# The threshold search of an expert-choice router, moved from a phase of its own into the batches of a linear attention

## What is computed

```python
# branch 1, linear attention (per sequence; then two layer norms and an MLP)
Q = elu(xn @ Wq + bq) + 1;  K = elu(xn @ Wk + bk) + 1;  V = xn @ Wv + bv
KV = einsum('bshd,bshm->bhdm', K, V)
Z  = 1 / (einsum('bshd,bhd->bsh', Q, K.sum(axis=1)) + 1e-6)
attn_out = einsum('bshd,bhdm,bsh->bshm', Q, KV, Z).reshape(b, s, 1024) @ Wo + bo
# branch 2, expert choice
scores = softmax(xn @ router_w + router_b)      # 4096 tokens x 8 experts
G, idx = top_k(scores.T, 256)                   # each expert takes its 256 best tokens
# gather, two matmuls with relu, weigh by G, add back to the tokens
x = x + s * silu(g)
```

## Time and profile before

| | us |
|---|---|
| median of 3 runs | 3729.77 (3727.99 to 3736.72) |
| the profiled execution | 3725.95 |
| its span, first to last instruction | 3724.1 |
| granted TensorE clock, mean over the span | 0.805 |
| PE busy over the span | 2474.6 (66%) |
| DVE busy over the span | 2064.1 (55%) |
| ACT busy over the span | 1371.2 (37%) |

### The profile page before, as it was taken

The page is one execution under the profiler, slowest core; times in us unless marked ns, Lnnn a source line. Parts: engine busy times, 40 slices in busy tenths (PEclk is TensorE's granted clock), DMA queues, the critical chain, the costliest instruction groups (busy, mean ns, idle before and its releaser), DMA issues. The chain is left out here.

```text
span 3724.1 us, 58202 instructions
## 1 busy us (share of the span) xinstructions
PE 2474.6 (66%) x19990; PEld 1767.7 (47%) x19990; DVE 2064.1 (55%) x4703; ACT 1371.2 (37%) x2383; POOL 825.8 (22%) x793
## 2 busy tenths in 40 slices
PE   5989941634250489804169999998615296968994
PEld 3655631522050488702145555557513275956773
DVE  4555566354919234264778888883345695442115
ACT  3444410322300023012148888883214332423432
POOL 0000001210057121073042000001344871113200
PEclk9999975775655699557579999998857697977997
DMA  5000000210021236310000000004410003731100
GB/s 170 1 1 0 0 2 14 65 28 3 0 54 37 46 122 206 89 41 4 19 28 20 1 1 1 1 1 146 146 35 25 20 0 114 221 95 36 32 0 28
DMA packets 156415, 172.87 MB, mean 46 GB/s; under 512 B 55333, under 2 KB 125738, under 8 KB 155594
## 3 DMA queue, kind: packets, MB, share of 16 engines
q1 hardware_dynamic: 135322, 127.39, 12.0%
q0 software_dynamic: 20912, 43.22, 3.9%
HBM read 124.61 MB, written 45.94 MB: 46 GB/s over the span
## 5 line engine op out<-in xcount | busy, mean ns | idle before, releaser
L2451 DVE CUSTOM_DVE_ANT_0 decayed_sd<-decayed_sc,decayed_decay 128x512 f32<-128x512 f32 x512 | 331.7, 686 | 86.0 <-PE decayed_sc L2328 85.8
L2406 ACT ACTIVATE decayed_pr<-decayed_sd,decayed_shift 128x512 f32<-128x512 f32 x512 | 339.0, 713 | 49.2 <-DVE decayed_shift L2458 49.0
L2340 PEld LDWEIGHTS decayed_tr<-all_ident,decayed_pr 128*128 128x128 f32 x2048 | 223.6, 140 | 175.1 <-ACT decayed_pr L2406 101.0
L2340 PE MATMUL decayed_tr<-all_ident,decayed_pr 128*128 128x128 f32 x2048 | 276.8, 278 | 11.0 <-ACT decayed_pt L2413 10.8
L450 PE MATMUL experts_up<-experts_xt,experts_w 128*128 128x256 f32 x1140 | 272.8, 386 | 0.0
L450 PEld LDWEIGHTS experts_up<-experts_xt,experts_w 128*128 128x128 f32 x1140 | 212.2, 195 | 24.7
L207 PE MATMUL norm_turned<-all_ident,norm_xn 128*128 128x128 f32 x128 | 35.7, 435 | 266.9 <-DVE norm_xn L143 266.9
L2465 DVE COPY decayed_pt<-decayed_tr 128x512 f32<-128x512 f32 x256 | 173.2, 685 | 2.6 <-PE decayed_tr L2340 2.6
L427 POOL DMA_DIRECT2D rows_out<-experts_y x121 | 87.4, 723 | 364.8 <-DVE experts_y L512 199.8
L376 POOL DMA_INDIRECT rows_in<-L_T,all_slot x128 | 149.5, 1168 | 83.0 <-issue 38.4
L684 PEld LDWEIGHTS moe_down<-moe_w,moe_h 128*128 128x128 f32 x1024 | 131.8, 192 | 56.3 <-issue 55.3
(11 more groups left out here) (508 smaller groups left out, 5578.5 us busy)
## 6 DMA issues: line engine op xcount, KB each, us to landing
experts_w<-in_L_experts SPq DMA_DIRECT2D x78, 384.0 KB, 3.3
experts_w<-in_L_experts SPq DMA_DIRECT2D x43, 579.0 KB, 4.0
experts_tok<-rows_in SPq DMA_DIRECT2D x121, 128.0 KB, 3.4
rows_out<-experts_y POOLq DMA_DIRECT2D x121, 128.0 KB, 3.4
fir_band<-bands SPq DMA_DIRECT2D x16, 768.0 KB, 7.4
rows_in<-linear_zero SPq DMA_DIRECT2D x43, 128.0 KB, 1.8
experts_w<-in_L_experts SPq DMA_DIRECT2D x8, 514.0 KB, 3.5
experts_b<-in_L_experts_b SPq DMA_DIRECT2D x43, 64.0 KB, 4.2
```

Source lines behind the costliest of these rows:

```text
L2340: last = pe.transpose(tr[u % TURNED][:, t * P:(t + 1) * P], pr[:, u % RING, t * P:(t + 1) * P], m.ident[:, :])
L2406: act.activation(pr[:, u % RING, :], sd[:, u % RING, :], ACT.Exp, bias=shift[:, u % RING:u % RING + 1]).then_inc(exp_ready, 1)
L2451: dve.tensor_tensor_reduce(out=sd[:, u % RING, :], in0=sc[h][:, :], in1=decay[:, qt, :], scale=1.0, scalar=-3.0e38, op0=ALU.mult, op1=ALU. ...
```

## The change

The search moves out of the choice phase. A class `Search` holds its buffers over both phases. The softmax and the first `propose` (L941 to L945 of the changed kernel) run on DVE before the first `join_q`, with the softmax's Exp first on ACT. The 15 counts and 15 decisions are spread over the 8 batches: one decision after V, one after the joins of the next Q; batch 0 has only the second. A decision of rounds 1 to 14 ends with the next round's `propose`; the last one does not. The counts are matmuls into the bank `y`, which is free until the output projection of the batch. All 8 batches are now written out, there is no loop and no register offset in the attention; `xb` and POOL's copies go, and PE takes the weights of K and V from `m.XNT`. SP stores `score` behind the zeroing. The choice phase starts at what was L1027.

```diff
+class Search:
+    ROUNDS, TRIED = 15, 3
...
+    def propose(self, dve):
+        self.link(dve.tensor_tensor(self.tried[:, :, :], self.found[:, :].unsqueeze(1).to_broadcast([P, self.TRIED, self.E]), self.bits[:, :, :],
+                                    ALU.bitwise_or))
+        for c in range(self.TRIED):
+            self.link(dve.tensor_tensor(self.marks[:, c], self.score[:, :, :], self.over(self.tried[:, c, :].bitcast(F32)), ALU.is_ge))
+        dve.tensor_reduce(self.part[:, :, :], self.marks[:, :, :, :].rearrange("p c t e -> p c e t"), AX, ALU.add).then_inc(self.part_ready, 1)
+    def count(self, pe, m, bank, n):
+        pe.wait_ge(self.part_ready, n + 1)
+        pe.matmul(bank[:, 0:self.TRIED * self.E], m.ones[:, :], self.part[:, :, :].rearrange("p c e -> p (c e)"), start=True, stop=True).then_inc(self.count_ready, 1)
+    def decide(self, dve, bank, n):
+        link = self.link
+        dve.wait_ge(self.count_ready, n + 1)
...
+        link(dve.tensor_single_scalar(self.bits[:, :, :], self.bits[:, :, :], 2, ALU.logical_shift_right))
+        if n + 1 < self.ROUNDS:
+            self.propose(dve)
...
         def rows(eng, body):
-            body(0, 0, False)
-            body(1, 1, False)
-            with eng.Fori(1, NB // 2 - 1) as i:
-                body(i * 2, 0, False)
-                body(i * 2 + 1, 1, False)
-            body(NB - 2, 0, False)
-            body(NB - 1, 1, True)
+            for b in range(NB):
+                body(b, b % 2, b == NB - 1)
...
             def body(b, slot, last_row):
-                pe.wait_ge(x_ready, b + 1)
                 for u in range(16):
+                    if u == 12 and b > 0:
+                        pe.wait_ge(y_step, b * 2)
+                        search.count(pe, m, y, 2 * b - 1)
...
-                    pe.matmul(proj[u % 2][:, :], xb[:, slot, t * P:(t + 1) * P], w[:, c * 512:(c + 1) * 512], start=True, stop=True).then_inc(kv_ps, 1)
+                    pe.matmul(proj[u % 2][:, :], m.XNT[:, b * 512 + t * P:b * 512 + (t + 1) * P], w[:, c * 512:(c + 1) * 512], start=True, stop=True).then_inc(kv_ps, 1)
...
                     last.then_inc(pair_ps, 1)
+                search.count(pe, m, y, 2 * b)
                 pe.wait_ge(kv_ready, b * GROUPS + GROUPS)
...
+            act.wait_ge(search.exp_in, 1)
+            act.activation(search.score[:, :, :], search.score[:, :, :], ACT.Exp).then_inc(search.exp_out, 1)
             act.wait_ge(preset, 2)
             split_q(0)
...
+                if b > 0:
+                    search.decide(dve, y, 2 * b - 1)
                 if not last_row:
                     join_q(b + 1, 1 - slot)
+                search.decide(dve, y, 2 * b)
...
             dve.memset(KV[:, :, :], 0.0).then_inc(preset, 1)
+            search.begin(dve, m)
             join_q(0, 0)
```

More of the change, by code:

```diff
@@ L907, in expert_choice_phase @@
+def expert_choice_phase(nc, phase, m, n_experts, capacity, search):
     E = n_experts
-    ROUNDS = 15
-    TRIED = 3
+    score, found = search.score, search.found
     with Scope(nc, phase) as s:
-        score = s.sb("score", [P, NT, E])
         mark = s.sb("mark", [P, NT, E])
-        marks = s.sb("marks", [P, TRIED, NT, E])
         equal = s.sb("equal", [P, NT, E])
@@ L951, in _ @@
             act.activation(which_t[:, :, :, :], turned[:, :].rearrange("p (a c b) -> p a c b", a=2, c=2), ACT.Copy).then_inc(turned_out, 1)
[L953 to L957, removed]
         @block.tensor
         def _(pe):
-            with pe.Fori(0, ROUNDS + 1) as i:
-                pe.wait_ge(part_ready, i + 1)
-                pe.matmul(count[:, 0:TRIED * E], m.ones[:, :], part[:, :, :].rearrange("p c e -> p (c e)"), start=True, stop=True).then_inc(count_ready, 1)
+            pe.wait_ge(part_ready, 1)
+            pe.matmul(count[:, 0:E], m.ones[:, :], part[:, :], start=True, stop=True).then_inc(count_ready, 1)
             pe.matmul(prefix[:, 0:NT * E], m.before[:, :], flat(equal), start=True, stop=True)
@@ L1210, in _, with linear_attention_phase @@
             sp.wait_ge(loaded, 16 * len(pairs))
-def linear_attention_phase(nc, phase, m, d, out, before):
+def linear_attention_phase(nc, phase, m, d, out, before, search):
     PAIRS, DH = 8, 64
@@ L1275, in _ @@
             sp.wait_ge(zeroed, 16 * (blocks_of_slots(12) + NT * P // SLOTS))
+            sp.wait_ge(search.score_ready, 1)
+            sp.dma_start(m.xn_rows[:, P:P + search.E].rearrange("(t p) e -> p t e", p=P), search.score[:, :, :]).then_inc(search.stored, 16)
+            sp.wait_ge(search.stored, 16)
         @block.gpsimd
@@ L1279, in _ @@
             pool.memset(zero[:, :], 0.0).then_inc(zero_ready, 1)
-            pool.tensor_copy(xb[:, 0, :], m.XNT[:, 0:512]).then_inc(x_ready, 1)
-            pool.tensor_copy(xb[:, 1, :], m.XNT[:, 512:1024]).then_inc(x_ready, 1)
-            with pool.Fori(1, NB // 2) as i:
-                for slot in range(2):
-                    pool.wait_ge(kv_ps, (i * 2 + slot - 1) * 16)
-                    pool.tensor_copy(xb[:, slot, :], m.XNT[:, bass.ds((i * 2 + slot) * 512, 512)]).then_inc(x_ready, 1)
         @block.tensor
@@ L2821, in build_layers @@
         m.router_bias = bias0[:, :]
[L2822 to L2824 removed]
+        with Scope(nc, "search") as a:
+            search = Search(a, 8, BATCH * SEQ // 16)
+            linear_attention_phase(nc, "linear", m, d, m.S, lambda loads: layer_norm_phase(
+                nc, "norm0", m, m.X, m.XNT, m.S, router=d["L0_router"], n_experts=8, loads=loads, stored=m.xn_rows), search)
+            expert_choice_phase(nc, "choice", m, 8, BATCH * SEQ // 16, search)
         with Scope(nc, "L0") as a:
```

88 lines of the change are left out of this document (40 added, 48 removed).

## The result

| | before | changed |
|---|---|---|
| median of 4 runs, us | 3730.32 (3727.99 to 3736.72) | 3697.97 (3695.36 to 3703.38) |
| the profiled execution, us | 3725.95 | 3697.87 |
| its span, us | 3724.1 | 3696.1 |
| last addition of `y`, starts at | 511.62 | 551.50 |
| choice's first comparison, starts at | 592.32 | 553.24 |

The changed kernel takes 0.9912 of the time before (95% interval 0.9895 to 0.9930), 32 us less where 49 were forecast. The median lies 1 us above the range. The same kernel, run again, took 3694.30 us (3690.73 to 3703.24), 0.9905 (0.9882 to 0.9928), with eleven half-clock stretches in its attention and the last addition at 551.91.

A forecast was written before the change was run, and what follows sets the result against it. PE bounds the attention and the choice is one chain, 78.96 us: -78.96 - 3.7 + 12.3 + 16.5 + 2.2 + 1.0 + 2 = -48.7 us, so a median of 3681 us, range 3669 to 3697.

The forecast's parts named there:

- loop written out: Attention's four looped batches: written out, each saves 0.93 us of register offsets, -3.7 us in all.
- start: Before the first Q joins: softmax and first proposal delay ACT's third projection, +1.0 us (0 to 6.5).
- counts (with the read): Second half of V, where PE paces: one more matmul of 0.31 us in seven batches, +2.2 us.
- delays, comparisons as before: Rounds delay Q's third projection by 2.05 us in six batches and `invert` by 2.35 in seven: 12.3 plus 16.5 us.
- clock: PE's 13 new gaps in Q and rows stages: one in ten loses full clock, 1.7 us each, +2 us.
- Together DVE is held for 3.95 us: One round on DVE: decision 1.03 us and proposal 2.87 us, taken from the old choice, hold it 3.95 us.
- the rival that every gap loses it: All 13 new PE gaps drop to half clock: 22 us in place of 2, total 3701 us; chance 0.13.
- the rival in which it stays through the rows stage: Slower than before: half clock lasts from `invert` to batch end, up to 18.8 us a batch, 3813 us; chance 0.02.
- Nothing hidden: Each of 13 rounds delays the attention by all its 3.95 us, start 6.5: total 3709 us; chance 0.06.
- all hidden: Slack elsewhere in the attention's batches absorbs the rounds' delays: total 3652 us; chance 0.05.
- signs named for being wrong in the sizes: Attention batches under 58 or over 63 us, where about 60.4 us each was forecast for batches 1 to 6.
- the loop gives nothing: Late instruction fetch takes back the 0.93 us a batch of the written-out attention loop: total 3685 us; chance 0.06.

The follow-up runs named there:

- written-out loop: The kernel before with only the attention's batches written out and K and V weights taken from XNT, search still in the choice phase: 3733.38 us, 1.0004.
- split decision: The changed kernel, decision after V moved behind Q's joins, the other cut: count read before `invert`, rest before the addition of `y`; 3650.49 us, 0.9792.
- both gaps filled: The changed kernel with only the last comparison linked, plus unused matmuls on PE: nine in the rows stage, eight before Q's third projection; 3678.93 us, one run.
- comparisons linked once: The changed kernel with only the last of a proposal's three comparisons raising the chain's semaphore: 3689.41 us in one run.
- the wait that fixes it: POOL's product of step n in layer 3 waits for DVE's of step n-6, added to four kernels: before 3726.68 us, changed 3687.06 us.
- one gap filled: The changed kernel with nine unused 128x128 matmuls on PE before its wait in the rows stage, batches 0 to 6: 3692.33 us, one run.
- the Q gap was gone: The changed kernel with the decision after V moved behind the joins of Q: 3681.48 us, 0.9876.

## Why the prediction was right or wrong

The direction, the leaving of the search from the path and both places of delay came as forecast. The loss in the attention, term by term, in us:

| term | forecast | measured | from |
|---|---|---|---|
| loop written out | -3.7 | -3.8 | written-out loop against the code of before with the same start (506.25 - 510.10) |
| start | +1.0 | +0.7 | batch 0 of the split decision (125.77) against that of the loop alone (125.10) |
| full clock earlier in the first Q | none | -1.5 | rest of the loop's -5.4; chance of the profile of before, which alone had it late |
| counts (with the read) | +2.2 | +1.9 | split decision, 0.30 a batch, 0.1 in batch 7 |
| delays, comparisons as before | +28.8 | +24.7 | both gaps filled: 2.09 in batch 0, 3.70 in four batches, 3.90 in batches 2 and 6 |
| two more linked comparisons | none | +3.1 | 13 x 0.24 |
| clock | +2 | +14.9 | changed kernel less both gaps filled, less 3.1 |
| sum | +30.3 | +40.0 (shown: 39.9) | |

**What bounds, and the choice.** This was right: PE's gaps end on ACT and DVE at the places named, ACT's third `expo` waits for the join, and the choice is off the path in full.

**The delays** were put too high by 0.35 us each; their term, 28.8 for a measured 24.7, by a seventh. The Q stage's is 1.71 and the rows stage's 2.00 with the comparisons as before, 1.95 and 2.23 with them linked. The round takes 3.77 us without the links in place of my 3.95 (150.15 to 154.16, less 0.24), since each instruction starts a little before the end shown for the one before it. In the Q stage, ACT's first `expo` also starts 0.36 us behind the last V addition, not 0.17, so that its slots cover 0.19 more. In the rows stage, the count is out 0.15 us earlier than I had it (7.48 us behind the start of the pairs, not 7.63). The 0.2 us more in the rows stage of batches 2 and 6 stand in every kernel that delays `invert`; their cause is open.

**The linked comparisons.** The step "Together DVE is held for 3.95 us" took the duration of three comparisons from a row of other code. This is a miss in reading the diff, 0.24 us a round.

**The clock** is the first of two steps that failed: "I take one gap in ten", 2 us for a measured 14.9. The Q gap loses it six times of six (0.9 to 1.4 us each), the rows gap three times of seven (1.6 to 2.8 us each), and the first Q stage once. In the second profile of the same kernel these were six of six, five of seven and none, so the Q stages lose it reliably and the rest varies. I had weighed, where one gap of two lost it, against "the work around these gaps is dense", and took the mild end; the rival that every gap loses it was nearer the truth, since 14.9 of its 22 us were lost. That its 3701 us lie near the measured 3698 is partly luck: 12.4 of the missing gain were lost elsewhere. What the trace showed was that a gap of 2.43 us can do it, and nothing in it said one in ten. The Trainium skill, TensorE: Matmul & The Clock Gate, HAM oscillation, was right in kind: in the case that it describes, with longer waits than these, each burst of matmuls behind a wait starts at the low clock, and here one burst or more did so in each of batches 0 to 6. The waits were 1.92 to 2.90 us, and each stretch at half clock was over after some 3.4 us, one after 6.8; the rival in which it stays through the rows stage had no batch. The length of the wait doesn't decide it alone: waits of 1.91 us in the Q stage lost the clock six times of six in the kernel with the comparisons linked once, and one of 1.95 us in the first Q projections didn't in the kernel with both gaps filled. What else does stays open.

**What is behind the attention** is the second step that failed: it had no term at all, and no reason for that was given. I took the 48.7 us at the end of the choice for 48.7 us at the end of the program. 12.4 got lost behind: 7.2 from the order of two engines in layer 3, shown by the wait that fixes it, and 4.2 in a phase that varies by 5 from profile to profile in unchanged code. With 9.6 in the attention and 1.4 won in the choice's tail this makes the 20.6 between the forecast's 48.7 and the profile's 28.1. The attention's 9.6 alone would have left the time inside the forecast's range, at 3691; it took both steps to leave it.

Nothing hidden, all hidden and slower than before did not occur. Of the signs named for being wrong in the sizes, a batch over 63 us, batch 1 alone met it (63.93), with two stretches at half clock. That the loop gives nothing seemed true by the end's time (1.0004) and is false: it gives 3.8 us in the attention, which the causal attention of layer 3 took back.

## What to carry to other kernels

Idle time of an engine hides work only where the work's own order lets it start at the beginning of the gap: put a chain of small steps where its input is long there and its result is not needed for its whole length, and cut it in pieces if no such place is long enough. A new wait of 2 us on PE costs its length and, in every batch here with two of them, 1 to 4 us more for the half clock behind it; move the cause, rather than counting on dense work around it. A gain of a few us in one phase should be looked for at the end of each later phase, since a shared resource can take it back in a phase that the change does not touch.

## What was not expected of the hardware

- A batch in the loop with register offsets takes 0.93 us longer than one written out, for the same work; written out, all take 55.65 us. Whether the offsets or the loop's branch cost it was not separated.
- Eight or nine added matmuls in a gap made the attention shorter, by 8.6 us with one gap filled, since less of it ran at half clock.
- The gap before a stretch that is itself paced by ACT (Q) lost the clock every time in both profiles of the changed kernel, and five times of six with the rows gap filled. The longer one before dense matmuls (rows) lost it in three and five of seven batches, and in two of seven when the Q gap was gone (one profile).
- DVE's product beside POOL's takes 1.34 us or up to 3.11, by which of the two began 0.1 us earlier.
- The activation table load stood before ACT's first wait (55.40 us), where I had put it behind, and the Exp ran at 57.88. The start cost 0.7 us, below the 1.3 of its chain.

```profile
55.40 1.28 ACT L1404 ACT_TABLE_LOAD   x1 [2.86 <-PEq L85]
...
57.88 0.42 ACT L1404 ACTIVATE search_score<-search_score 128x256 f32<-128x256 f32 x1 [1.20 <-DVE search_score L928]
```
